# Spreading the indirect DMAs of a routed transformer kernel: waits on exponentials and on slot tiles

## The reference, cut to what matters

```python
xn = (x - mu) * rsqrt(var + eps) * gamma + beta
probs = softmax(xn @ Wr + br)                 # 8 experts
scores, idx = top_k(probs, 2)
full = relu(xn @ W1[e] + b1[e]) @ W2[e] + b2[e]     # 128 -> 512 -> 128, for the chosen two
out = x + sum(scores * (full[idx] - c[idx] + c_total))
```

## Time and profile before

| | |
|---|---|
| time of the runs (3) | 2293.94 us median, 2292.66 to 2307.22 |
| span of the profiled execution | 2374.1 us (the page gives no other time of it) |
| PE busy | 1915.4 us, 81% |
| DVE busy | 1428.9 us, 60% |
| ACT busy | 1180.8 us, 50% |
| POOL busy | 1135.4 us, 48% |
| mean granted clock of PE | 0.875 |
| a1; m1a; a2 (from the span's start) | 1160 to 1426; 1426 to 1670; 1670 to 2089 |
| m1b | 2089 to 2374, of which the last gathers from 2325 |
| indirect DMAs | 128 gathers, 128 scatters, 16.79 MB |

### The profile page before, as it was taken

How to read it: one execution, slowest core, us unless ns; L and a number is a source line. 1 busy time by engine, 2 the same in 40 slices (tenths; PEclk the granted TensorE clock), 3 DMA queues, 4 the chain that set the end, 5 groups by cost and what they waited for, 6 DMA issues and landing times. The chain is left out here.

```text
span 2374.1 us, 43139 instructions
## 1 busy us (share of the span) xinstructions
PE 1915.4 (81%) x14694; PEld 1329.8 (56%) x14694; DVE 1428.9 (60%) x4140; ACT 1180.8 (50%) x2785; POOL 1135.4 (48%) x2002
## 2 busy tenths in 40 slices
PE   7978999978776888786899888889488887678891
PEld 6866888866332343343455447778234443267781
DVE  6997999955663555475788844323478886333232
ACT  3435666653443677553566544334156764443340
POOL 2534555543354555345567672522666545124225
PEclk9998999999796999898899969899568977589995
DMA  8000000000000000000000005556000000045572
GB/s 259 1 1 1 1 1 1 2 1 0 1 1 1 1 2 1 1 1 1 2 2 2 10 29 154 157 176 194 18 20 6 2 1 24 14 129 176 169 205 78
DMA packets 93945, 109.50 MB, mean 46 GB/s; under 512 B 12945, under 2 KB 76833, under 8 KB 93601
## 3 DMA queue, kind: packets, MB, share of 16 engines
q1 hardware_dynamic: 85536, 89.96, 12.7%
q0 software_dynamic: 8192, 16.79, 2.4%
HBM read 78.14 MB, written 28.57 MB: 45 GB/s over the span
## 5 line engine op out<-in xcount | busy, mean ns | idle before, releaser
L1998 ACT ACTIVATE a2prob<-PS 128x512 f32<-128x512 f32 x256 | 143.9, 598 | 109.5 <-PE PS L1767 82.8
L1535 DVE TENSOR_REDUCE a2mx<-PS 128x4 f32<-128x1024 f32 x128 | 156.0, 1219 | 61.0 <-PE PS L1743 43.1
L2449 POOL DMA_INDIRECT gy<-rows_out,pos x96 | 90.7, 944 | 165.2 <-DMA rows_out<-m1byo 62.7
L1535 DVE TENSOR_REDUCE a1mx<-PS 128x6 f32<-128x768 f32 x128 | 121.8, 952 | 51.4 <-PE PS L1750 50.8
L2001 ACT ACTIVATE a0prob<-PS 128x1024 f32<-128x1024 f32 x128 | 127.3, 1028 | 50.8 <-PE PS L1767 50.5
L1998 ACT ACTIVATE a1prob<-PS 128x384 f32<-128x384 f32 x256 | 116.4, 490 | 72.5 <-PE PS L1767 71.0
L241 DVE SCALAR_TENSOR_TENSOR cv_y<-cv_gl,k_conv_w,cv_y 128x256 f32<-128x256 f32 x320 | 131.3, 477 | 19.6 <-ACT cv_y L349 10.2
L280 PE MATMUL PS<-cv_rT,cv_diag 128*128 128x256 f32 x640 | 142.2, 382 | 0.0
L1360 POOL TENSOR_SCALAR_AFFINE_SELECT a1prob<-a1prob 128x256 f32<-128x256 f32 x256 | 97.8, 411 | 78.7 <-ACT a1prob L1998 78.0
L280 PEld LDWEIGHTS PS<-cv_rT,cv_diag 128*128 128x128 f32 x640 | 121.3, 191 | 16.9
L2480 DVE TENSOR_SCALAR m1ahid<-PS,m1awr 128x256 f32<-128x256 f32 x92 | 40.3, 479 | 148.3 <-PE PS L2577 95.4
(11 more groups left out here) (528 smaller groups left out, 5402.5 us busy)
## 6 DMA issues: line engine op xcount, KB each, us to landing
m1awr<-in_wtab SPq DMA_DIRECT2D x46, 514.0 KB
m1bwr<-in_wtab SPq DMA_DIRECT2D x46, 514.0 KB
rows_in<-cv_blank SPq DMA_DIRECT2D x46, 128.0 KB, 2.1
m1axin<-rows_in SPq DMA_DIRECT2D x46, 128.0 KB
rows_out<-m1ayo SPq DMA_DIRECT2D x46, 128.0 KB
m1bxin<-rows_in SPq DMA_DIRECT2D x46, 128.0 KB
rows_out<-m1byo SPq DMA_DIRECT2D x46, 128.0 KB
X<-in_x SPq DMA_DIRECT2D x4, 512.0 KB, 6.2
```

Of the source, the lines that this page charges most:

```text
L1535: v.tensor_reduce(mx[:, 2 * j:2 * j + 2, :], MB[:, :, 0:SEG * seg_len].rearrange("p h (s n) -> p h s n", n=seg_len), AX.X, ALU.max).then_i ...
L1998: act.activation(prob[:, h % RING, 0:n_prob], SB[(b * NH + h) % NSB][:, 0:n_prob], ACT.Exp, scale=scale).then_inc(s["exp"], 1)
L2449: pool.indirect_dma_start(gy[:, (u * HALF + t) % GY, k, :], None, ys[u], bass.IndirectOffsetOnAxis(ap=pos[:, u, k, t:t + 1], axis=0))\
```

## The change

Nothing is computed otherwise; indirect DMAs are issued at other times. In a2 the tail has no gathers in the prologue: all 16 row tiles are gathered in batches 0 to 5, and each of the two gathers waits for an exponential, the second for that of one head later. The first-half scatters in a1 and a2 each wait for the exponential of the head before. In the sparse stages the gathers of half 0 wait for one more slot tile per row tile, and the second-half scatters wait for two slot tiles more than before.

```diff
-    TAIL_FIRST = 6
-    TAIL_AT = {(i // 3, 3 + 5 * (i % 3)): TAIL_FIRST + i for i in range(HALF - TAIL_FIRST)}
+    TAIL_AT = {(i // 3, 3 + 5 * (i % 3)): i for i in range(HALF)}
...
-            def tail_gather(t):
+            def tail_gather(t, b, h):
                 finished(pool, s["tcm"], t - GY)
                 for k in range(2):
+                    pool.wait_ge(s["exp"], b * NH + h + k)
                     pool.indirect_dma_start(g["gy"][:, t % GY, k, :], None, g["ys"][1],
...
                     if tail and (b, h) in TAIL_AT:
-                        tail_gather(TAIL_AT[b, h])
+                        tail_gather(TAIL_AT[b, h], b, h)
...
                     if route and sent(b, h) < sent(b, h + 1) <= 2 * HALF:
+                        pool.wait_ge(s["exp"], b * NH + h)
                         route.scatter(pool, 0, sent(b, h) // 2, sent(b, h) % 2)
...
-            if tail:
-                for at in range(TAIL_FIRST):
-                    tail_gather(at)
             if route:
                 route.clear(pool)
...
-                    if tail and b == 0 and h in (1, 5):
-                        tail_combine(4 + h // 4)
...
-                    if tail and j >= PAIRS - 3:
-                        tail_combine(j - PAIRS + 3)
                 prepare_minus(0, 0)
-                if tail:
-                    tail_combine(3)
...
                 for t in range(HALF):
                     finished(pool, s["cm"], u * HALF + t - GY)
+                    if u == 0:
+                        pool.wait_ge(s["down"], COMBINE - 2 + t)
                     for k in range(2):
...
             for at in range(2 * HALF):
-                pool.wait_ge(s["down"], 8 + at // 3)
+                pool.wait_ge(s["down"], 10 + at // 3)
                 route.scatter(pool, 1, at // 2, at % 2)
```

## The result

The changed kernel took 2309.91 us (median of 12 runs, 2294.94 to 2318.95), the kernel before 2301.90 beside it (12 runs, 2292.66 to 2307.22). The ratio is 1.004 with a 95% interval of 1.0022 to 1.0057: 5 to 13 us slower, where 2293 and "no change" were forecast. The profiled execution of the changed kernel took 2318.95 us by its own time, its span is 1.7 us less. So it belongs to the timed runs. That of the kernel before did not: its span was 72 us above their median, and on which chip it was taken is not on record.

The account below looks back on a forecast made before the run. Undisturbed, the sparse stages run at PE's pace; in a2 PE is busy for 298 of 368 us. The terms +3 +2 +1 -7 = -1 on the median of 2293.94 gave 2293, with a range from 2240 to 2314.

Parts of the forecast that it names:

- The stalls: Five places, in a2, m1a and m1b, where runs of indirect DMAs disturb PE's pace: 21, about 10 or 9 us each.
- the question: Whether the timed runs have the five stalls; taken as likelier that most of the stall belongs to the profiled execution.
- A: The forecast: stalls in a2, m1a and m1b are in the profiled execution only; 2293, own range 2275 to 2312; chance 0.55.
- B: Stalls in a2, m1a and m1b are in every run; 48 us faster, 2246, between 2225 and 2270; chance 0.32.
- The sum of the stalls, 59 us: a2 21, about 10 for each run of scatters and 9 for each run of gathers in m1a and m1b.
- the 21 us that it left over: Whole profiled execution: without the stalls its span would be 2315, 21 us above the timed median.
- The reading of the stalls: In a2, m1a and m1b PE's signals reach others late while indirect DMAs run back to back beside a busy PE.
- Part 1: Prologue of a2: 12 gathers leave POOL, four combines leave DVE; gain 0, or 2.8 us if the cover were gone.
- Part 2: Batches 3 to 5 of a2: 6 row tiles move in; cost between 0 and 9.4 us, taken as 3.
- Part 3: First-half scatters: 0 in a1; in a2 waits cost 0 to 3 us in each of two batches, taken as 2.
- Parts 4 and 5: Sparse stages: second-half scatters cost 1 us in all; gathers of half 0, two per tile, gain 6 to 7.
- Rival C: Batches 0 to 5, 12 and 13 of a2: POOL held behind ACT, DVE's cast late; 24 us slower, 2318; chance 0.10.

Follow-up runs that it names:

- f1: Kernel before with all 16 tail row tiles gathered in batches 0 to 5 of a2, without waits for exponentials: 2385.69 us against 2380.40, 1.0022.
- f2: Kernel before without the 32 first-half scatters of a2, on a stalling chip: 2348.76 us, 0.9877.
- f3: Kernel before with first-half scatters waiting for the exponential of the head before, in a2 one at every head: 2370.63 us, 0.9954.
- f4: Kernel before with the tail's gathers in a2 at heads 3, 6 and 9 instead of 3, 8 and 13: 2386.12 us, 1.0018.
- k2: Kernel before with only the sparse stages changed, on a stalling chip: 2338.18 us, 0.9832.
- e0_same: The kernel before, unchanged, profiled and timed again on a quiet chip: 2301.90 us, 1.0026.
- k1_after: The changed kernel, all parts, timed again on a stalling chip: 2318.94 us, 0.9760 against the kernel before.
- e1_tail: Kernel before with only the tail's part: all 16 row tiles gathered in batches 0 to 5 of a2 behind exponentials: 2305.28 us, 1.0037.
- h1: The changed kernel, all parts, timed again on a quiet chip: 2320.49 us, 1.0075 against the kernel before.
- h2: The changed kernel without the tail's part, on a quiet chip: 2310.15 us, 1.0031 against the kernel before.
- e2_att_scat: Kernel before with only the first-half scatters of a1 and a2 waiting for the exponential of the head before: 2308.11 us, 1.0047.
- h3: Kernel before with only the sparse stages changed, on a quiet chip: 2301.72 us, 0.9980.
- set 1: First set of experiments, on a quiet chip: the kernel before unchanged, then each of the change's three parts alone; kernel before 2300.11 us.
- h4_no_scat: Kernel before without the 32 first-half scatters of a2, on a quiet chip: 2310.72 us, 1.0021.
- l0: The changed kernel without the tail's part, on a stalling chip: 2312.18 us, 0.9733 against the kernel before.

## Why the prediction was wrong

**The stalls (the question, and rivals A and B).** The prediction asked whether the timed runs have them, and answered by where a profiled execution is special. That step failed. The gap of 80 us between span and median has the size of the difference between the two kinds of chip, and no price of recording is needed for it. On a stalling chip the timed runs of the kernel before take 2380, and the profiles there of kernels that keep a part of it (f1, f2, f3, f4, k2) show its stalls in that part. On a quiet one its timed runs take 2300 and its profile (e0_same) has none. The kernel before itself was not profiled in a stalling set; that the earlier trace rows came from such a chip is inferred from its length and its stalls. After the change the gap shrank to 7 us, where A had some 30. The rule of the Trainium skill that was drawn on (page "NOTIFIC — the notification-queue block", section "Overflow: three behaviours, one of which stalls the engine") speaks of recording, and e0_same was recorded without a stall. Recording alone doesn't make them. Whether it has a part on a stalling chip no run here shows, since there is a span for timed runs too.

**The sum of the stalls, 59 us.** It was too small, and the argument from the 21 us that it left over fell with it. Stage by stage against e0_same, m1a is 23.9 us longer (220.4 against 196.5 from first to last copy), m1b 18.1 (216.1 against 198.0) and the end of a2 35.2 (93.9 against 58.7). That is 77 of the 82 us between the spans, so next to nothing is spread over other stages. In m1a the sum had some 10 us for the run of scatters, read from one tile. Another tile behind it, the one between these two copies of ACT, took 9.8 us against 5.5 in e0_same:

```profile
1514.13 0.38 ACT L2654 ACTIVATE m1ayo<-PS 128x256 f32<-128x256 f32 x1 [2.25 <-PE PS L2588]
1523.88 0.38 ACT L2654 ACTIVATE m1ayo<-PS 128x256 f32<-128x256 f32 x1 [2.20 <-PE PS L2588]
```

In a2 it stopped at the batch of 44.8 us, which takes 20.8 in e0_same, and left out the two behind it, which ran at a clock of 0.67 and 0.50 and take 16.2 and 13.5 us there:

```profile
2038.60:2058.30 19.70, 17.12 (x152) 7.95 (x151) 11.66 (x18) 11.05 (x21) 0.00 (x0) 0.67 0.00 1
2058.30:2077.40 19.10, 17.04 (x123) 7.12 (x121) 3.08 (x9) 10.71 (x22) 0.00 (x0) 0.50 0.01 1
```

A's number came close by luck, because the comparison ran on a quiet chip. B's mechanism is real on the others: it gave 48 us, and k1_after measured 58. It started from the stalls as mis-sized above. The rest of 2.4 us that it left of each run of scatters is about what k2_sparse shows (m1a 199.0 us, against 196.5 in e0_same).

**The reading of the stalls** (indirect DMAs back to back beside a busy PE, the prologue free of it) was right as far as it went. k2_sparse and k1_after remove them by moving the DMAs apart and nothing else. That it is PE's signals that are late rests on the earlier trace rows and was not tested by a run. The spacing has a dose: none left at one scatter per two heads, 31 us instead of 44.8 at one per head, a rest at three per slot tile. What it lacked was the condition under which they appear.

**Part 1, prologue: 0.** Measured 1.2 us back in e1_tail's profile against e0_same, inside its bound of 2.8; by the medians over all profiles nearly 4, above it.

**Part 2, the tail in batches 3 to 5: +3, bound 9.4.** Mis-sized. Its two items can be seen in e1_tail, 1.6 us more wait of the cast and 2.0 of combines where one interval grows by 4.3. That the first is a cost f4 leaves in doubt. Over all profiles, from the first to the twelfth addition of a2, the median is 236.9 us in the five with the tail's part and 229.5 in the 14 others: 7.4 us, less the 4 of the prologue. But the sum was cut to a third of its bound without a reason from a row. Timed runs say +5 (e1_tail against before) and +10 (h1 against h2). That the waits for exponentials cost next to nothing was right: POOL came late to most of them (6 of 32 gathers waited in e1_tail, 3 in the changed kernel), and f1 without them was slower than before as well, by the same 5 us.

**Part 3, first-half scatters: +2.** Mis-sized, and by another mechanism than the one priced: +8 (e2_att_scat), and +8 between h3 and h2. The prediction looked for work queued behind POOL. The loss is PE's clock in the stage's last batches, to which the sum gave no price, though the earlier trace rows had it at 0.65 and 0.57. Four windows of 4 us each, e0_same, and then e2_att_scat:

```profile
1992.00:1996.00 4.00, 3.06 (x40) 1.61 (x36) 3.21 (x6) 2.40 (x5) 3.01 (x4) 1.00 0.16 49
1996.00:2000.00 4.00, 3.07 (x34) 1.20 (x31) 2.84 (x5) 2.55 (x5) 3.08 (x4) 0.84 0.19 60
2000.00:2004.00 4.00, 4.00 (x32) 2.40 (x32) 1.71 (x3) 2.69 (x6) 2.52 (x3) 0.50 0.17 54
...
2008.00:2012.00 4.00, 3.01 (x40) 1.50 (x32) 0.72 (x4) 3.23 (x7) 0.00 (x0) 1.00 0.01 2
```

```profile
1986.00:1990.00 4.00, 3.77 (x52) 1.95 (x48) 2.88 (x4) 3.43 (x8) 2.23 (x3) 1.00 0.10 33
1990.00:1994.00 4.00, 3.07 (x32) 1.04 (x28) 2.80 (x4) 2.47 (x5) 2.15 (x3) 0.77 0.16 52
1994.00:1998.00 4.00, 3.28 (x25) 1.74 (x22) 2.16 (x2) 2.68 (x5) 1.91 (x2) 0.50 0.06 17
...
2022.00:2026.00 4.00, 3.41 (x26) 1.14 (x26) 0.00 (x0) 2.49 (x5) 1.91 (x2) 0.50 0.10 33
```

Both fall from 2.4 to 1.2 GHz after a stretch at the upper level. With the burst PE is back within 8 us here (in e1_tail, which has it too, a later stretch at the lower level lasted 17); with spaced scatters it stays at the lower for more than 30.

**Parts 4 and 5, the sparse stages: +1 and -7.** On quiet chips the two together measured -2 and -4, each with an interval that takes in 0. No load was late, as forecast; but the -7 counted contention that the quiet chip doesn't have: its tiles beside the 12 gathers take 4.0 to 4.2 us. That credit was read from stalls of the other kind of chip.

By medians, +5, +8 and -2 make +11 from set 1, and the changed kernel measured +8 and +15. The forecast's -1 took 3, 2 and -6 for them.

**Rival C** ended on the right side, with the wrong mechanism: behind the prologue of a2 DVE's cast waited 13.1 us for POOL, against 7.7, below the 15 that would have shown it.

## What to carry to other kernels

A profile and the times beside it may have been taken under different conditions. When their gap is many times the spread of the runs, profile the unchanged kernel again, beside its own time, before anything is explained. Before a sum of stalls is compared with such a gap, add up whole stages, the slower stretch behind a stall included. Spacing back-to-back indirect DMAs beside a busy PE was worth 58 to 66 us in 2380 where such stalls exist and cost 4 to 15 where they don't; its part in the sparse stages alone was worth 38 and cost nothing measurable. An engine's idle time ahead of an instruction is not its price: taking 4 to 6 us of it away in f4 made nothing faster. In a stage that PE paces, look at the granted clock of the stretch before and after an edit: an order with fewer stalls can be slower by the clock alone.

## What the runs showed that was not expected

- The kernel before takes 71 to 80 us more in 2300 (3.1 to 3.5%) in one set than in another, with POOL's scatters the same to the nanosecond (23 of 954/958/1007 ns in both profiles). What differs is open; chip 6 was slow both times.
- In the profiles on quiet chips the end of a2 is 8 us shorter with 23 scatters back to back beside PE than with no scatter at all (58.7 against 66.9 us), with a granted clock of 0.88 instead of 0.50 to 0.61. In timed runs h4_no_scat is 5 us above the kernel before, which is not clear of noise. The cause of the clock's turn is open; l0 shows that it can go the other way without the burst.
